# Transformer block on one core: in the last attention group the middle query tiles are computed first, and the middle tokens' share of the last feed-forward network is moved beside the outer tokens' attention

## What is computed

```python
x = x + L0_attn(layernorm(x))        # attention over the 256 channels
x = x + L0_ffn(layernorm(x))         # silu(gate) * up, inner width 1024
x = x + L1_attn(layernorm(x), ...)   # causal, 32 query heads, 8 key/value heads, head size 64, rope
x = x + L1_ffn(x)                    # two ternary "bitlinear" products around a gelu
# bitlinear(x, w):
#   xn = (x - mean) / sqrt(var + 1e-6)
#   x_hat = clip(xn * 128 / absmax, -128, 128) * absmax / 128      (per token)
#   y = x_hat @ (sign(round(w / mean|w|)) * mean|w|).T
# h = gelu(bitlinear(x, w_fc));  result = bitlinear(h, w_proj),  inner width 1024
```

## Time and profile before

| | |
|---|---|
| median of 3 runs | 632.56 us (632.03 to 632.80) |
| the profiled execution | 630.89 us |
| its span in the profile | 628.9 us |
| mean granted TensorE clock over the span | 0.976 |
| TensorE matmuls busy | 563.0 us, 90% |
| VectorE / ScalarE / GpSimd busy | 461.7 / 434.7 / 450.0 us |
| DMA transposes (queue q1) | 79.3% of 16 engines' span |

### The profile page before, as it was taken

One profiled execution on the slowest core, in us unless ns is written; L12 is line 12 of the kernel. 1 busy time (PEld: TensorE's weight loads), 2 busy tenths in 40 slices (PEclk: granted clock), 3 DMA queues, 4 the chain that ended last, 5 costly groups with the idle time before them and its releaser, 6 DMA issues.

```text
span 628.9 us, 16324 instructions
## 1 busy us (share of the span) xinstructions
PE 563.0 (90%) x6880; PEld 484.8 (77%) x6880; DVE 461.7 (73%) x764; ACT 434.7 (69%) x601; POOL 450.0 (72%) x373
## 2 busy tenths in 40 slices
PE   5999999987889999999999999999999868774896
PEld 4878888966678888888888888888889757663475
DVE  4686757767768878878877887887888756519696
ACT  0624311268788898889879889888888897701894
POOL 3033436529989998998998999999999787724121
PEclk9999999999999999999999999999999999966799
DMA  9160004009999999999999999999999999950001
GB/s 288 49 200 0 2 22 88 2 22 164 192 171 196 183 197 193 188 194 215 191 190 190 199 205 193 193 187 190 192 199 193 184 191 207 186 108 0 1 26 43
DMA packets 317192, 91.75 MB, mean 146 GB/s; under 512 B 305984, under 2 KB 316224, under 8 KB 317120
## 3 DMA queue, kind: packets, MB, share of 16 engines
q1 hardware_dynamic: 311680, 86.66, 79.3%
q10 hardware_dynamic: 5440, 4.06, 2.4%
HBM read 13.11 MB, written 1.05 MB: 23 GB/s over the span
## 4 chain that ended last, share of the span: by engine, by line
PE 33%; POOL 23%; DVE 13%; DMA 13%; SPq 6%; ACT 6%; issue 5%; POOLq 0%; ACTq 0%; DVEq 0%
POOL p_lo L478 17%; PE PS L1154 11%; DMA pT_lo<-p_lo 10%; DVE small L1006 4%; PE PS L1413 4%; SPq L382 4%; PE PS L1287 3%; POOL roped L467 3%; SPq L386 3%; DMA pT_hi<-p_hi 2%; PE PS L1264 2%; PE PS L1269 2%; PE PS L1265 2%; ACT probs L656 2%; PE PS L1433 2%
## 5 line engine op out<-in xcount | busy, mean ns | idle before, releaser
L478 POOL TENSOR_TENSOR p_lo<-probs,p_hi 128x1280 f16<-128x1280 f32 (+7 forms) x128 | 303.6, 2391 | 35.2 <-DMA pT_lo<-p_lo 20.5
L656 ACT ACTIVATE probs<-PS,small 128x640 f32<-128x640 f32 (+7 forms) x256 | 173.6, 743 | 43.2 <-DVE small L1006 40.1
L1006 DVE TENSOR_REDUCE small<-PS 128x2 f32<-128x1280 f32 (+7 forms) x128 | 172.8, 1351 | 22.7 <-PE PS L1413 22.1
L665 ACT CAST p_hi<-probs 128x1280 f16<-128x1280 f32 (+7 forms) x128 | 145.4, 1159 | 4.8 <-DMA pT_hi<-p_hi 4.7
L1433 PE MATMUL PS<-v_hi,pT_hi 128*128 128x65 f16 x1152 | 78.9, 195 | 1.6 <-DMA pT_hi<-p_hi 1.6
L1437 PE MATMUL PS<-v_lo,pT_hi 128*128 128x64 f16 x1152 | 78.9, 195 | 0.0
L1433 PEld LDWEIGHTS PS<-v_hi,pT_hi 128*128 128x128 f16 x1152 | 74.1, 99 | 3.3 <-issue 1.1
L1413 PE MATMUL PS<-k_hi,q_hi 64*128 64x512 f32 (+3 forms) x384 | 74.0, 381 | 1.2 <-ACT probs L656 1.2
L1437 PEld LDWEIGHTS PS<-v_lo,pT_hi 128*128 128x128 f16 x1152 | 72.6, 98 | 0.4
L1413 PE MATMUL PS<-k_hi,q_lo 64*128 64x512 f32 (+3 forms) x384 | 66.1, 339 | 0.0
L1413 PE MATMUL PS<-k_lo,q_hi 64*128 64x512 f32 (+3 forms) x384 | 66.0, 339 | 0.0
(11 more groups left out here) (188 smaller groups left out, 1330.6 us busy)
## 6 DMA issues: line engine op xcount, KB each, us to landing
wgu_nat<-L_ffn_w_gate_up SPq DMA_DIRECT2D x2, 1024.0 KB, 9.6
wo_nat<-L_attn_wo ACTq DMA_DIRECT2D x8, 256.0 KB, 3.4
wkq_nat<-L_attn_wq ACTq DMA_DIRECT2D x6, 256.0 KB, 4.2
x<-L_attn_x SPq DMA_DIRECT2D x4, 256.0 KB, 3.8
wdn_nat<-L_ffn_w_down SPq DMA_DIRECT2D x1, 1024.0 KB, 11.3
wfc_nat<-L_ffn_w_fc SPq DMA_DIRECT2D x1, 1024.0 KB, 6.7
wpj_nat<-L_ffn_w_proj SPq DMA_DIRECT2D x1, 1024.0 KB, 9.7
pT_hi<-p_hi SPq DMA_TRANSPOSE x64, 5.6
```

The source lines that it names most:

```text
L478: nc.gpsimd.tensor_tensor(p16_lo[G % 2][:, cols], probs[G % 2][:, cols], p16_hi[G % 2][:, cols], ALU.subtract).then_inc(p_lo_done, 1)
L656: nc.scalar.activation(probs[G % 2][:, start:start + w], PS[:, src:src + w], ACT.Exp, bias=nmax[:, 4 * (G % 2) + u:4 * (G % 2) + u + 1]).t ...
L665: nc.scalar.copy(p16_hi[G % 2][:, cols], probs[G % 2][:, cols]).then_inc(p_hi_done, 1)
L1006: nc.vector.tensor_reduce(nmax[:, first:first + 2], both_heads(G, part), AX.X, ALU.max, negate=True).then_inc(nmax_done, 1)
```

## The change

**Order of the last group.** `of_step` gives group 7 another order: pairs of steps alternate between the two pairs of heads, r 0 and 1 (tiles 4, 3, 5 and 2, the middle ones) for both pairs of heads come in steps n = 0 to 3, r 2 and 3 (tiles 6, 1, 7 and 0, the outer ones) in n = 4 to 7. The last group has its own table of side jobs and its own load of output weights, into tiles of its own (`wo_nat_last`, `wo_hi_last`, `wo_lo_last`), at n = 0 instead of n = 4; they are split at n = 3 instead of at the end.

```diff
             g, n = G // 8, G % 8
+            if g == NG - 1:
+                return g, n, n // 2 % 2, 2 * (n // 4) + n % 2
             return g, n, n // 4, n % 4
 ...
-            r = G % 4
+            r = of_step(G)[3]
             return 4 - r if part else 5 + r
 
 ...
+        LAST_JOBS = {0: ("q1t0", "q1t1", ""), 1: ("", "", "ot2"), 2: ("", "", ""), 3: ("ot3", "wo1", ""),
+                     4: ("wo2", "", ""), 5: ("ot0", "wo0", ""), 6: ("wo3", "", ""), 7: ("ot1", "po1", "po2")}
+        LAST_WO = (1, 2, 0, 3)
+        TAIL_TILES = (2, 3, 4, 5, 0, 1, 6, 7)
+
+        def wo_count(gg, j):
+
+            return 4 * gg + (LAST_WO.index(j) if gg >= NG - 2 else j) + 1
+
-        RING += [(STEPS, "pv"), (STEPS + 1, "pv"), (STEPS + 1, "ot2"), (STEPS + 2, "pv"), (STEPS + 2, "ot3")]
+        RING += [(STEPS, "pv"), (STEPS + 1, "pv"), (STEPS, "ot2"), (STEPS + 2, "pv"), (STEPS + 2, "ot3"),
+                 (STEPS + 2, "po0"), (STEPS + 2, "po3")] + [(STEPS + 3, f"pj{t}") for t in range(NT)]
 ...
             def load_wo(g):
+                wo_rows = wo_b[2 * g * P:2 * (g + 1) * P, :].rearrange("(c p) n -> p c n", p=P)
+                if g == NG - 1:
+                    act.wait_ge(wkq_split, NG)
+                    act.dma_start(wo_nat[1][:], wo_rows).then_inc(wo_last_landed, 16)
+                    return
                 if g:
                     act.wait_ge(wo_split, g)
 ...
-                if n == 2 and g:
+                if n == (1 if g == NG - 1 else 2) and g:
                     split_wo_low(g - 1)
-                if G == STEPS - 1:
-                    split_wo_low(NG - 1)
+                if n == 3 and g == NG - 1:
+                    split_wo_low(g)
                 p_low(G, 1)
```

```diff
             side(STEPS, "pv")
+            pe.wait_ge(exp_done, 4 * STEPS)
             side(STEPS + 1, "pv")
-            side(STEPS + 1, "ot2")
-            pe.wait_ge(exp_done, 4 * STEPS)
-            out_project(NG - 1, 1, 1)
-            out_project(NG - 1, 2, 2)
+            x_transposes(3, 0, 4)
+            side(STEPS, "ot2")
+            fc(0)
             side(STEPS + 2, "pv")
             side(STEPS + 2, "ot3")
-            out_project(NG - 1, 0, 0)
-            out_project(NG - 1, 3, 3)
-
-
-            x_transposes(3, 0, 4)
-
 ...
             fc(1)
-            x_transposes(3, 1, 4)
-            for t in range(NT):
-                if t + 2 < NT:
-                    fc(t + 2)
+            side(STEPS + 2, "po0")
+            side(STEPS + 2, "po3")
+            z_transposes(0)
+            fc(2)
+            fc(3)
+            pe.wait_ge(gelu_done, 4)
+            x_transposes(3, 1, 0)
+            for t in range(1, NT):
                 z_transposes(t)
-                if t >= 1:
-                    pj(t - 1)
-            pj(NT - 1)
+                side(STEPS + 3, f"pj{t - 1}")
+                if t + 3 < NT:
+                    fc(t + 3)
+            side(STEPS + 3, f"pj{NT - 1}")
```

```diff
-            for t in range(NT):
+            def z_factor(t):
+                z_rstd(t)
+                pool.wait_ge(z_rstd_done, t + 1)
+                pool.wait_ge(z_done, t + 1)
+                nc.gpsimd.tensor_scalar(bit[:, 7, t:t + 1], bit[:, 5, t:t + 1], bit[:, 10, t:t + 1],
+                                        ngam[:, 1:2], ALU.mult, ALU.mult).then_inc(z_factor_done, 1)
+
+            rstd_half(0)
+            z_mean(0)
+            z_mean(1)
+            z_factor(0)
+            y_centre(4)
+            y_centre(5)
+            z_mean(2)
+            rstd_half(1)
+            z_mean(3)
+            z_factor(1)
+            for t in range(4, NT):
                 z_mean(t)
-                if t:
-                    z_rstd(t - 1)
-            z_rstd(NT - 1)
+                z_factor(t - 2)
+            z_factor(NT - 2)
+            z_factor(NT - 1)
```

```diff
             p_high(STEPS - 1, 1)
-            split_wo_high(NG - 1)
-            oT_high(NG - 1, 2, side_bank(STEPS + 1, "ot2"))
-            oT_high(NG - 1, 3, side_bank(STEPS + 2, "ot3"))
+            act.wait_ge(moments_done, 3 * NT + 4)
+            nc.scalar.activation(y_nmean, moments[:, 3, 0:8:2], ACT.Identity, scale=-1.0).then_inc(y_mean_done, 1)
+            act.wait_ge(y_mean_done, 1)
+            for t in range(4):
+                nc.scalar.activation(y[:, t, :], x[:, TAIL_TILES[t], :], ACT.Identity,
+                                     bias=y_nmean[:, t:t + 1]).then_inc(y_centred, 1)
+            nc.scalar.activation(col(58), s_sum[:, 0:1], ACT.Gelu)
 ...
+            oT_high(NG - 1, 2, side_bank(STEPS, "ot2"))
             gelu_of(0)
             centre(0)
+            oT_high(NG - 1, 3, side_bank(STEPS + 2, "ot3"))
+            squares(0)
+            gelu_of(1)
+            centre(1)
+            squares(1)
+            z_high(0)
+            gelu_of(2)
+            centre(2)
+            gelu_of(3)
+            squares(2)
             for c in range(KC):
-                x_high(3, 1, c, 6 + c)
-            for t in range(NT):
-                if t:
-                    centre(t)
+                x_high(3, 1, c, 2 + c)
+            z_high(1)
+            for t in range(3, NT):
+                centre(t)
                 if t + 1 < NT:
                     gelu_of(t + 1)
-                if t:
-                    z_high(t - 1)
+                z_high(t - 1)
                 squares(t)
             z_high(NT - 1)
```

200 lines of the change are left out of this document (106 added, 94 removed).

## The result

The change takes the median from 632.29 to 616.42 us (612.59 to 617.08, 4 runs); the ratio is 0.974, with a 95% interval of 0.9696 to 0.9783. The forecast was 619.3, with a range of 614.6 to 622.4: the sign and the range held, and the gain was 15.9 us instead of 13.3. The profiled execution took 617.08 us with a span of 615.3, against a forecast span of 615.6.

What follows compares the result with a forecast made beforehand. Bound by the transfer chain in attention, then one string into a TensorE-bound loop of 4.35 us a tile. z_transposes(2) at 586.6 plus 29.3, less 0.3, gave span 615.6; 13.3 us off the median gave 619.3, range 614.6 to 622.4.

Steps and rivals of the forecast that it cites:

- step 3: Behind pv(62): y transposes 2.1 us at the lower clock, copy 0.6, split 0.6, fc(0) 3.4, ending at 561.2.
- step 4: pv(63) to fc(3): no wait for the last low half, TensorE unbroken from 564.4, ending at 573.6.
- step 7: Seam before the loop: z_transposes(1), pj(0), fc(4), clock low for most of the tile, from 579.0 to 586.6.
- Step 1: Group 7: output products fill transfer waits; moved splits, 0 to 2.5 us, taken as 0; attention's end unchanged.
- the forecast's own sign of being wrong: Attention ending more than 2 us elsewhere; also fc(0) behind pv(63), or a loop period over 4.5.
- rival 2: Group 7's steps get longer by both splits in front of low halves: up to 2.5 us, 621.8; chance 0.10.
- Step 2: First half of y, made beside attention, ready at 553.1 before pv(62) ends at 554.6; 1.5 us margin hides it.
- Steps 5 and 6: TensorE idles 2.2 us for gelu(3) before y's second transposes, then 2 us for z_low(0) before z_transposes(1).
- the clock stays up: Rival at the seam: no fall of TensorE's clock, step 7 ends at 583.9, time 616.6 us; chance 0.16.
- Step 8: From z_transposes(2) to the end: 29.3 us as before, less 0.3 for the factor leaving VectorE; span 615.6.
- The port: VectorE's scaling of y may wait for GpSimd's p_low; y then ready at 553.8, still before 554.6, adding nothing.
- tells 0.2% from nothing: Assumed resolution of a measurement of this kernel, 1.3 us, behind chances of faster 0.95, same 0.01, slower 0.04.

Runs made afterwards that it cites:

- y_on_dve: Changed kernel with VectorE instead of ScalarE centring the first four tiles of y: 618.55 us, ratio 0.9801.
- seam_filled: Changed kernel with unread matmuls in TensorE's two seam waits: 614.79 us, ratio 0.9727; C (first z transposes to those of tile 2) 14.24 instead of 16.54.
- factor_dve: Changed kernel with the factor of the result made on VectorE again instead of GpSimd: 616.48 us, ratio 0.9757.
- fc_late: Changed kernel with the first y transposes and fc(0) put behind pv(63) and ot3 again: 623.81 us, ratio 0.9873.
- before_filled: Kernel before, with unread matmuls in TensorE's three idle stretches behind attention: 628.40 us, ratio 0.9950.
- seam_gelu_first: seam_filled with ScalarE making gelu(3) ahead of the centring of tile 2: 615.38 us, ratio 0.9742; changed kernel in the same set 615.53.
- all_filled: seam_filled with further unread matmuls behind pv(61), before step 62's last low-half products and before fc(0): 616.51 us, ratio 0.9753.

## Why the prediction was right, step by step

The forecast put the mark, the start of `z_transposes`(2), at 586.6; it is at 585.88. That it fits within 0.7 is in part luck: attention ended 1.9 us late, and the steps behind it were together 2.6 shorter than forecast (1.3 in step 3, 0.4 in step 4, 0.9 in step 7).

| step | forecast | measured | |
|---|---|---|---|
| 1. last issue of the SyncE queue | 554.5 | 556.10 | 1.6 late |
| 2. y ready against the end of `pv`(62) | 1.5 before | 1.1 before | right |
| 3. end of `pv`(62) to end of `fc`(0) | 6.6 | 5.3 | `fc`(0) mis-sized |
| 4. from there to the end of `fc`(3) | 12.4 | 12.0 | right |
| 5. idle for gelu(3) | 2.2 | 2.16 | right |
| 6. idle for `z_low`(0) | 2 | 2.10 | right, but not by its terms |
| 7. `z_transposes`(1) to (2) | 7.6 | 6.71 | between the clocks, as said |
| 8. from there to the end | 29.0 | 29.4 | the factor gave nothing |

- **Step 1** said that attention ends where it did. At 1.9 us late it nearly met the forecast's own sign of being wrong, 2 us. In the profiled execution the last low half was issued 1.6 us later. That is not shown to be the change: the distance from step 55 to step 63 on GpSimd is 51.1 us in both profiled executions, so 1.3 of the lag was there when group 7 began, and the second execution of the changed kernel has `pv`(62) end at 555.33, 1.2 earlier. Over the twelve traces of the changed kernel and its variants that end wanders from 553.4 to 557.9. The doubled splits leave room for a part of a microsecond of cost; rival 2, with its 2.5, did not come.
- **Step 2** held, with its cover as thin as given. The wait of VectorE for GpSimd, set aside as "nothing in the sum", was there (0.50 instead of 0.17), and y was ready 1.1 us before it was needed. y_on_dve shows what lies behind that margin.
- **Step 3** took `fc`(0) at 1.2 GHz, 3.4 us; it took 2.03 since the clock had come back by then. This term was mis-sized by 1.4. How much of `fc`(0) the low clock covers differs from trace to trace: it took 1.88 to 3.01 us over the traces of the kernels that have it in front of `pv`(63). It is also the place that no fill improved in the end.
- **Steps 5 and 6**, the two new waits that TensorE meets, came at their places, with their releasers and within 0.1 us. They rested on adding up ScalarE's and VectorE's queues instruction by instruction. The sum of step 6 has a gap, though: 569.3 and its terms 2.5, 2.8, 2.3 and 1.2 make 578.1, where it says 578.9. The trace has the missing 0.8. VectorE was still at the moments of the two tiles before, and began the last addition (570.33) 0.83 us behind the end of `po3` (569.50).
- **Step 7.** The clock fell and came back inside the tile, as taken; the rival "the clock stays up" is what seam_filled makes, and there C is 2.3 us shorter, priced at 2.7. That the clock would fall at all rested on one earlier case, at 592; behind the idle stretch that ends near 173 us of the same trace it had stayed up. So this term came out well by luck as much as by reasoning.
- **Step 8.** The 0.3 for the factor was wrong: the loop's period is TensorE's, and factor_dve shows VectorE idle for 1.25 us of a tile even with the factor on it. I had set the period by TensorE and still credited VectorE's saving.
- **The port.** The Trainium skill, "SBUF — State Buffer", "Who interferes with whom", has, for VectorE instructions that also use the ports shared with GpSimd, an exclusive lock held by whoever comes first. By the rows ahead of the forecast only GpSimd had been seen to wait. The trace agrees for the other order now: 0.50 us and 2.98 us, each ending with GpSimd's instruction. GpSimd waited once more as well: the mean of z(1) took 0.66 us (567.95) instead of 0.26 and ended just behind VectorE's scaling of z(0). Neither delayed TensorE in that trace.
- **The median** gained 15.9 where the profiled executions differ by 13.8 (630.89 to 617.08). The executions of the changed kernel spread over 4.5 us, and the profiled one was its slowest, while that of the kernel before was its fastest. So the match of the spans (13.6 us of gain against 13.3) is the better test of the sum, and "tells 0.2% from nothing" was too fine: four executions gave an interval of 0.4% to either side.

Of the 15.6 us that the stretch from `pv`(62) to the z transposes of tile 2 lost, fc_late gives 7.8 to the place of the y transposes and `fc`(0). The rest was not taken apart: the two output products in step 63, the scaling of y beside attention and the order of the tail. How much of either half is the clock is open as well; before_filled shows 3 us for two of the three low stretches, in the kernel before.

The best version is seam_filled, 614.79 and 0.9727 in a set where factor_dve, the changed kernel in all but one small instruction, has 616.48 and 0.9757. In the third set its relative seam_gelu_first could not be told from the changed kernel, so of the 2.3 us in the trace the medians confirm 1.7 once and 0.2 once; all_filled, with the same two fills and more, shows none.
